# One decoder layer on one core: batch 0's third norm cut into pieces, and two groups of weighted products moved in TensorE's order

## The reference

```python
x = x + attn(layernorm(x))                       # 16 heads, causal softmax
# cross-attention: per head two softmaxes of half-heads of 4, keys = 154 context tokens
a1 = softmax(q1 @ k1.T * s); a2 = softmax(q2 @ k2.T * s)
x = x + ((a1 - lam * a2) @ v * (1 - 0.2)) @ w_out.T + b_out
# feed-forward, bit_linear: round(x * 127 / max|x|) per token, weights rounded to -1, 0, 1
h = bit_linear(layernorm(x), w1)                 # 128 -> 512
h = silu(depthwise_conv1d(h, conv_w, conv_b))    # 3 taps over time
x = x + bit_linear(h, w2)                        # 512 -> 128
```

## Time and profile before

| what | before |
|---|---|
| median of 3 runs | 312.63 us (312.25 to 312.78) |
| the profiled execution's own time | 311.38 us |
| its span, first to last instruction | 309.6 us |
| mean granted TensorE clock | 0.999 |
| busy in the span: PE, DVE, ACT, POOL | 91%, 70%, 63%, 46% |

### The profile page before, as it was taken

The page is one execution under the profiler, slowest core; times in us unless marked ns, Lnnn a source line. Parts: engine busy times, 40 slices in busy tenths (PEclk is TensorE's granted clock), DMA queues, the critical chain, the costliest instruction groups (busy, mean ns, idle before and its releaser), DMA issues.

```text
span 309.6 us, 6618 instructions
## 1 busy us (share of the span) xinstructions
PE 282.8 (91%) x2446; PEld 179.1 (58%) x2446; DVE 216.5 (70%) x481; ACT 195.3 (63%) x484; POOL 143.8 (46%) x252
## 2 busy tenths in 40 slices
PE   0799699899999989989899999899999999999994
PEld 0567566566666668655566676445454553447763
DVE  3758877886766651778577746987888779447854
ACT  1587477667777770787677731567777767625344
POOL 3704577894577771584446510059119173000331
PEclk9999999999999999999999999999999999999999
DMA  7920000000000000000000000000000000000001
GB/s 279 307 89 3 0 3 1 2 2 0 3 2 3 0 2 0 2 3 0 2 0 2 4 3 0 2 0 0 2 0 1 3 0 3 0 0 2 0 25 44
DMA packets 4835, 6.17 MB, mean 20 GB/s; under 512 B 834, under 2 KB 3650, under 8 KB 4676
## 3 DMA queue, kind: packets, MB, share of 16 engines
q1 hardware_dynamic: 4516, 5.42, 5.0%
q10 hardware_dynamic: 288, 0.33, 0.3%
HBM read 5.23 MB, written 0.52 MB: 19 GB/s over the span
## 4 chain that ended last, share of the span: by engine, by line
PE 73%; DVE 12%; ACT 8%; issue 3%; DMA 2%; SPq 0%; ACTq 0%
PE bank L724 64%; PE bank L797 5%; ACT pr L546 4%; DVE nmax L1370 3%; DVE qk L1415 3%; DMA pT<-in_wv 2%; ACT pT L546 1%; PE bank L949 1%; PE bank L1037 1%; ACT pT L677 1%; DVE pT L1386 1%; DVE stats L1301 1%; DVE xn L1314 0%; DVE onT L1335 0%; DVE km L1324 0%
## 5 line engine op out<-in xcount | busy, mean ns | idle before, releaser
L646 ACT ACTIVATE pT<-bank 128x512 f32<-128x512 f32 (+1 forms) x80 | 44.5, 600 | 25.6 <-PE bank L724 25.1
L339 POOL TENSOR_SCALAR pr<-pr,pinv 128x256 f32<-128x256 f32 (+2 forms) x96 | 45.4, 489 | 28.7 <-DVE pinv L1378 28.6
L1415 DVE TENSOR_REDUCE qk<-bank 128x4 fp32r<-128x616 f32 x64 | 48.9, 795 | 13.6 <-PE bank L724 13.4
L546 ACT ACTIVATE pr<-bank,nmax 128x256 f32<-128x256 f32 (+2 forms) x96 | 44.3, 479 | 18.2 <-DVE nmax L1370 17.9
L724 PE MATMUL bank<-qs 64*128 64x256 f32 (+3 forms) x256 | 49.4, 469 | 4.1 <-ACT pr L546 3.7
L1370 DVE TENSOR_REDUCE nmax<-bank 128x2 f32<-128x512 f32 (+2 forms) x48 | 31.6, 687 | 14.5 <-PE bank L724 14.4
L724 PE MATMUL bank<-pT,v_sb 128*64 128x128 f32 (+2 forms) x320 | 38.4, 385 | 0.0
L339 POOL TENSOR_SCALAR pT<-pT,pinv 128x512 f32<-128x512 f32 x32 | 21.7, 692 | 23.6 <-DVE pinv L1378 23.6
L1386 DVE COPY pT<-bank 128x512 f32<-128x512 f32 (+1 forms) x32 | 30.3, 948 | 1.1 <-PE bank L797 1.1
L724 PEld LDWEIGHTS bank<-pT,v_sb 128*64 128x64 f32 x320 | 21.1, 136 | 14.1 <-issue 10.8
L724 PE MATMUL bank<-km,qk 64*128 64x308 f32 x128 | 27.7, 366 | 1.2 <-DVE qk L1415 1.1
(11 more groups left out here) (190 smaller groups left out, 576.4 us busy)
## 6 DMA issues: line engine op xcount, KB each, us to landing
pT<-in_wqk SPq DMA_DIRECT2D x1, 1024.0 KB, 6.5
cw_sb<-in_cw SPq DMA_DIRECT2D x1, 768.0 KB, 8.2
x_sb<-in_x SPq DMA_DIRECT2D x2, 256.0 KB, 5.6
pT<-in_wv SPq DMA_DIRECT2D x1, 512.0 KB, 7.5
wo_sb<-in_wo SPq DMA_DIRECT2D x1, 512.0 KB, 6.9
out<-x_sb SPq DMA_DIRECT2D x8, 64.0 KB, 1.6
onT<-in_consts ACTq DMA_DIRECT2D x1, 256.0 KB, 6.7
pT<-in_xwk SPq DMA_DIRECT2D x1, 256.0 KB, 7.5
```

The source lines that it names most:

```text
L339: nc.gpsimd.tensor_scalar(d, d, pinv[:, t, a:a + 1], 1.0, ALU.mult, ALU.mult).then_inc(norm_done, 1)
L546: nc.scalar.activation(prob[r][:, a, at:at + w], bank[:, SP[k % 2] + a, at:at + w], ACT.Exp, bias=nmax[:, t, a:a + 1], accum_out=psum[:, t ...
L646: nc.scalar.activation(px[rows, i, :], bank[rows, (ST0, ST1)[i % 2], :], ACT.Exp, scale=SD ** -0.5).then_inc(xexp_done, 1)
L1415: nc.vector.tensor_reduce(m, s_in, AX.X, ALU.max, negate=True).then_inc(round_done, 1)
```

## The change

Three edits, none of which adds or takes away a computation.

1. DVE, group 6: the four `bn_stats` are issued two behind the maximum of `j` = 0 and two behind that of `j` = 1, instead of four behind `j` = 1. The four subtractions are issued two behind `j` = 3 and two behind `j` = 4, instead of four behind `j` = 4, and the largest absolute value stands at `j` = 5 (where group 6 has no maximum) instead of right behind them.
2. TensorE, group 7: `cross_weighted(6, 1)` stands behind the second scores instead of behind the fourth.
3. TensorE, behind group 7: `cross_weighted(7, 1)` stands ahead of `conv(0, [0])`, and `turn_last_sums(1)` ahead of the second tap instead of behind it.

```diff
@@ the eight groups, TensorE
                 if more:
                     next_max(G, 1)
+                else:
+                    cross_weighted(G - 1, 1)
                 cross_scores(G, 2)
                 if more:
                     next_max(G, 2)
                 cross_scores(G, 3)
-                if G >= 1:
+                if G >= 1 and more:
                     cross_weighted(G - 1, 1)
@@ behind the groups, TensorE
             first, second = range(0, HALF), range(HALF, NT)
-            conv(0, [0])
             pe.wait_ge(xexp_done, 20 * NG)
             cross_weighted(B * NG - 1, 1)
-            conv(0, [1])
+            conv(0, [0])
             turn_last_sums(1)
-            conv(0, [2])
+            conv(0, [1, 2])
             turn_att(3, first)
             turn_att(3, second)
@@ DVE: tile_stats and centre are split in two functions each
             def tile_stats(ts):
                 for t in ts:
                     link(nc.vector.bn_stats(stats[:, t, :], x_sb[:, t, :]))
+                spreads(ts)
+
+            def spreads(ts):
                 settle()
                 for t in ts:
                     link(nc.vector.bn_aggr(mv[:, t, :], stats[:, t, :]))
@@
             def centre(ts):
                 for t in ts:
                     link(nc.vector.tensor_scalar(xn[:, t, :], x_sb[:, t, :], mv[:, t, 0:1], None, ALU.subtract))
+                largest(ts)
+
+            def largest(ts):
                 settle()
                 link(nc.vector.tensor_reduce(amax[:, ts[0]:ts[-1] + 1], xn[:, ts[0]:ts[-1] + 1, :], AX.X, ALU.max,
                                              apply_absolute_value=True))
@@ the eight groups, DVE
+                    if G == 6 and j in (0, 1):
+                        for t in range(HALF * j, HALF * j + HALF):
+                            link(nc.vector.bn_stats(stats[:, t, :], x_sb[:, t, :]))
                     if G == 6 and j == 1:
-                        tile_stats(range(NT))
-                    if G == 6 and j == 4:
-                        centre(range(NT))
+                        spreads(range(NT))
+                    if G == 6 and j in (3, 4):
+                        for t in range(HALF * (j - 3), HALF * (j - 3) + HALF):
+                            link(nc.vector.tensor_scalar(xn[:, t, :], x_sb[:, t, :], mv[:, t, 0:1], None, ALU.subtract))
+                    if G == 6 and j == 5:
+                        largest(range(NT))
```

## The result

| | before | changed |
|---|---|---|
| median | 312.2 us (10 runs, 311.05 to 313.66) | 310.2 us (10 runs, 309.44 to 311.2) |
| ratio | | 0.9944 (95% interval 0.9926 to 0.9961) |
| the profiled execution: its own time, span | 311.38, 309.6 | 311.2, 309.4 |
| mean granted TensorE clock | 0.999 | 0.993 |

The change made the kernel faster by 0.56%, 1.75 us by the ratio. The predicted shift, 1.45 us or a ratio of 0.9954, lies inside the measured interval. But the difference of the two medians is 2.00 us. Taken from the 312.2 of this timing, 1.45 us gives 310.75, which lies in the range. So the miss of 1.0 us (311.2 against 310.2) has two parts of like size: the level that the shift was subtracted from, 0.43 us, and the shift, 0.55 us by the medians.

A forecast was written before the change was run, and what follows sets the result against it. The prediction took TensorE, busy for 91% of the span, as the bound, with three idle stretches to fill. Its terms, 0 + 0.7 + 0.75 = 1.45 us, took the median 312.63 to 311.2 us, range 310.6 to 312.0.

The forecast's parts named there:

- the range: Whole kernel: forecast time 310.6 to 312.0 us, from the DVE edit's full gain to the edit behind group 7 alone.
- What bounds the kernel: Whole kernel: TensorE, busy for 91% of the span; its idle places in the region of the change were to be filled.
- the three idle stretches: TensorE's waits in group 6 (0.61 us), group 7 (0.69) and before `turn_att` (0.76), 2.06 us in sum.
- Edit 1, 0: DVE, group 6: the same work stays ahead of reduction 5, so TensorE waits as long; gain 0 us.
- The rival from the Trainium skill: DVE, group 6: breaking up work also removes the wait before 258.70; 310.6 us in all, chance 0.06.
- Edit 2, 0.72 by the steps: Group 7: weighted products fill TensorE's wait for ACT, scores 6 start at 267.91 instead of 268.63; taken as 0.7 us.
- Edit 3, 0.73 by the steps: Behind group 7: last sums are turned earlier, so `turn_att` comes at 277.20 instead of 277.93; taken as 0.75 us.
- The prediction's reading of the rule: Behind group 7: two fewer changes of matmul shape would give 0.2 us more; left out of the sum.
- a shift of 1.45 takes the median 312.63 to 311.2: Whole kernel: the summed gain of 1.45 us subtracted from the earlier runs' median, giving the forecast of 311.2 us.
- 0.1 us of scatter: High end of the range, 312.0 us: the edit behind group 7 alone, with this much allowed for scatter.
- time won ahead of `turn_att` should arrive at the end whole: Behind 277.93 TensorE's chain runs unbroken for 8.34 us from 278.58 and everything there hangs on `turn_att`.

The follow-up runs named there:

- late_spreads: Changed kernel with the aggregates and variance of batch 0's norm behind DVE's reduction 5 instead of reduction 4; 308.81 us, ratio to before 0.9905.
- early_stats: Changed kernel with batch 0's four statistics issued earlier, in DVE's idle time from group 5 on; 309.92 us, ratio to before 0.9932.
- both_pe: Kernel before with the two TensorE edits (group 7 and behind it), without the DVE edit; 309.9 us, ratio to before 0.9936.
- again: Changed kernel timed once more, nothing altered, beside the kernel before on the same chip; 309.79 us, ratio 0.9926 (0.9906 to 0.9945).
- only_group7: Kernel before with only the group 7 edit, weighted products behind the second scores; 311.14 us, ratio to before 0.9980.
- The hold: TensorE held at its end until the eight outputs have landed; ratio to before 0.9941 on the changed kernel, 0.9958 with early statistics.

## Why the prediction was right or wrong

**What bounds the kernel: right.** Time was won at two of the three idle stretches, and late_spreads and early_stats show that it could be won at the third.

**Edit 1, 0: right.** 0.00 us in the stretch (2.81 us from reduction 3 to 5, both times). The rival from the Trainium skill, Perfetto Trace Analysis, Optimizing Scalar/DVE Operations, that breaking up work may complete some of it sooner, did not happen here, since what the waiting reduction stood behind remained the same. early_stats is the case in which its idea works: the same pieces, moved into DVE's idle time, shorten group 6 by 0.76 us.

**Edit 2, 0.72 by the steps, taken as 0.7: right, 0.65 measured** (0.66 from scores 0 to scores 6). The small difference arises ahead of the rest products: they start 3.65 us behind scores 0 where the steps said 3.59. That is where the steps had the longer of the two new waits for ACT.

**Edit 3, 0.73 by the steps, taken as 0.75: right, 0.80 measured.** The wait of 0.76 is gone, and TensorE's own steps fell from 6.18 - 0.76 = 5.42 to 5.38 us. `conv(0, [0])` takes 275.50 - 274.27 = 1.23 us where it took 1.31, now that no change to the weighted products' shape follows. The Trainium skill, TensorEngine Tiling (Array Packing), Key Properties, says that a change of tiling mode drains TensorE. The trace fits this, with 0.08 us here; no row shows the drain itself. The prediction's reading of the rule would have put 0.2 on edit 3, which is too much. The two groups of products take 2.09 us (272.18 to 274.27) where the steps said 2.00; exponential 9 ends only at 273.14, so a short wait for it is likely. From the last sums to `turn_att` it is 2.06 where the steps said 2.14.

**The first step that failed: "a shift of 1.45 takes the median 312.63 to 311.2", in its level.** The level was the median of three executions, and the range gave it "0.1 us of scatter". The ten runs of the same timing have 312.2, 0.43 us lower, and the 126 of the experiments 311.7, 0.9 us lower. The warning stood in the table before: the profiled execution's own time was 1.25 us under the median of the three. The prediction mentioned that distance and then carried it along as if it were fixed. Two things were found that vary with the same code: the low clock in self-attention (0.6 us between the medians) and the tail (by 1.0 us in the changed kernel).

**The second: "time won ahead of `turn_att` should arrive at the end whole".** Up to the last compute instruction it holds in every kernel, 28.83 to 28.91 us from `turn_att`. Behind it the prediction put all change at nothing, and the tail isn't fixed. It was 2.7 to 2.9 us in three of three profiles of the kernel before, and 1.97 us in two of three of the changed one. The times, too, won more than the stretches: the ratios of the changed kernel (0.9944, 0.9926, 0.9942) and of both_pe (0.9936) all lie below the 0.9954 of a shift of 1.45 us, and the interval of again excludes it. Executions of like clock say the same: 312.07 to 310.2 with a low mean clock, 311.43 to 309.2 without, 1.8 and 2.2 us.

For the 0.3 to 0.9 us that this is more than 1.45, a shorter tail in part of the executions is the candidate, as it would give 0.8 us in each of them. It is not shown. only_group7 speaks against reading it off one profile: its tail was 1.92 us as well, yet its twelve executions won only 0.6 us, no more than its stretch. The hold did not bring the time either. So this part stays open.

That 311.7 - 1.45 comes to the 310.2 that was measured is luck, not an account: the 310.2 was timed beside 312.2, and all 22 executions of the changed kernel have a median of 309.97.

## What to carry to other kernels

Cutting work into pieces frees a waiting instruction only if a piece leaves the queue ahead of it or falls into idle time; count what stands ahead of it, in sum, before and after. Work that fills one engine's wait is worth what the next wait leaves of it: step through the other engine's order until both meet again. And a shift is known better than a level: where the runs of the kernel before are few and one differs from the others by as much as the change is worth, state the ratio and widen the range for the level. When the profiles of two kernels are compared, look first whether they had reached the same instruction at the same time ahead of the change.

## What the runs showed of the hardware

The same instruction stream ran with a 3.4 us stretch of the lower granted clock in nine of 18 profiles, each time between 37.2 and 42.1 us. Between two matmuls around it the time was 11.48 to 11.61 us with it and 10.08 to 10.09 without. TensorE had passed the same idle times ahead of it in both cases (0.38 us before the first of these matmuls); the nine executions with the stretch had come there by 33.16 us, the nine without at 33.31 us or later. By the mean clock, 75 of 126 executions of the kernel before had it, with a median of 312.07 us against 311.43.

The issue of a 64 KB output on SyncE's queue took 0.33 us in most cases. Nine profiles have a 16 KB packet of instructions between the last outputs. In these the slowest output took 2.4 to 3.5 us from issue to landing, and in seven of the nine the issue of one of the last two outputs took 0.96 to 2.04 us. In the nine others no output took over 1.6 us to land and no issue over 0.43 us. The tail behind the last compute instruction was 2.74 to 3.30 us with the packet and 1.91 to 1.98 without it and without the hold. What decides when that packet comes is open.
